# Two mixture layers computed by routed expert groups in place of all experts for all tokens, around a causal attention layer

## The reference

```
x = x + 0.5 * mixture(norm(x))      # router over 4 experts, the best 2 count
x = x + attention(norm(x))          # causal, linear (no softmax), 16 heads of 16
x = x + 0.5 * mixture(norm(x))      # the same weights again

mixture(h):
  g = softmax(layer_norm(h) @ router_w.T); top2_w, top2_idx = top_k(g, 2), renormalized
  hid = relu(layer_norm(h @ w1[e]) * ln_g + ln_b)         # per expert, 256 -> 512
  out = sum over the two experts of top2_w * (hid @ w2[e])    # 512 -> 256
  return layer_norm(out) * on_g + on_b
```

## Time and profile before

| | us |
|---|---|
| device time, median of 3 runs (lowest, highest) | 1240.89 (1239.82, 1241.86) |
| the profiled execution: span from first to last instruction | 1236.4 |
| TensorE matmul busy, 8694 matmuls | 1140.2 (92%) |
| VectorE busy | 948.3 (77%) |
| GpSimd busy | 672.0 (54%) |
| ScalarE busy | 512.8 (41%) |

### The profile page before, as it was taken

The page is one execution under the profiler, slowest core; times in us unless marked ns, Lnnn a source line. Parts: engine busy times, 40 slices in busy tenths (PEclk is TensorE's granted clock), DMA queues, the critical chain, the costliest instruction groups (busy, mean ns, idle before and its releaser), DMA issues.

```text
span 1236.4 us, 25066 instructions
## 1 busy us (share of the span) xinstructions
PE 1140.2 (92%) x8694; PEld 731.9 (59%) x8694; DVE 948.3 (77%) x2150; ACT 512.8 (41%) x878; POOL 672.0 (54%) x1039
## 2 busy tenths in 40 slices
PE   4669799999999999889999999889999999999996
PEld 4335456656566566656666666556566665666664
DVE  5678787887978878657777777578879787797875
ACT  4353324233342424456665666442333424334131
POOL 2365546454565544498778777543555654546360
PEclk9789989999999999999999999899999999999998
DMA  9002000000000000000000000000000000000000
GB/s 286 4 1 69 1 1 2 1 2 1 0 0 0 1 2 1 19 18 15 11 13 18 17 18 18 1 2 2 17 1 18 1 19 18 0 17 1 19 18 17
DMA packets 29037, 20.69 MB, mean 17 GB/s; under 512 B 7812, under 2 KB 27784, under 8 KB 28808
## 3 DMA queue, kind: packets, MB, share of 16 engines
q1 hardware_dynamic: 24112, 18.36, 5.4%
q10 hardware_dynamic: 4824, 1.07, 0.5%
HBM read 11.03 MB, written 4.19 MB: 12 GB/s over the span
## 4 chain that ended last, share of the span: by engine, by line
PE 48%; DVE 19%; issue 16%; POOL 10%; ACT 4%; DMA 2%; DVEq 1%; ACTq 0%; POOLq 0%
PE bank L1547 7%; PE bank L1549 6%; PE bank L1548 6%; DVE area L674 5%; DVE area L682 4%; PE bank L1532 4%; PE bank L1534 4%; PE bank L1533 4%; DVE area L655 4%; PE bank L1506 4%; POOL area L487 3%; PE bank L1555 2%; PE bank L1557 2%; PE bank L1556 2%; DMA betas<-in_L_ffn_ln_b_dram 2%
## 5 line engine op out<-in xcount | busy, mean ns | idle before, releaser
L1256 ACT ACTIVATE area<-area 128x512 f16<-128x512 f32 x256 | 160.9, 630 | 387.9 <-DVE area L674 386.1
L1547 PE MATMUL bank<-w2h,area 128*128 128x256 f16 x1024 | 281.3, 275 | 12.9 <-DVE area L693 7.2
L1548 PE MATMUL bank<-w2l,area 128*128 128x256 f16 x1024 | 280.5, 274 | 0.0
L1549 PE MATMUL bank<-w2h,area 128*128 128x256 f16 x1024 | 280.5, 274 | 0.0
L674 DVE SCALAR_TENSOR_TENSOR area<-area,betas,bank 128x512 f32<-128x512 f32 x256 | 189.9, 743 | 46.0 <-PE bank L1534 37.6
L682 DVE SCALAR_TENSOR_TENSOR area<-area 128x512 f16<-128x512 f32 x256 | 188.7, 737 | 20.3 <-ACT area L1256 17.1
L1532 PE MATMUL bank<-hTh,w1h 128*128 128x512 f16 x512 | 195.5, 382 | 6.7 <-DVE area L674 6.7
L1533 PE MATMUL bank<-hTl,w1h 128*128 128x512 f16 x512 | 195.1, 381 | 0.0
L1534 PE MATMUL bank<-hTh,w1l 128*128 128x512 f16 x512 | 194.9, 381 | 0.0
L696 DVE SCALAR_TENSOR_TENSOR area<-bank,coef,area 128x256 f32<-128x256 f32 x192 | 92.1, 482 | 79.3 <-PE bank L1549 78.1
L487 POOL TENSOR_TENSOR area<-area 128x512 f16<-128x512 f32 x96 | 119.9, 1274 | 45.1 <-ACT area L1300 44.9
(11 more groups left out here) (233 smaller groups left out, 2109.6 us busy)
## 6 DMA issues: line engine op xcount, KB each, us to landing
X<-in_L_attn_x_dram SPq DMA_DIRECT2D x8, 512.0 KB, 7.1
area<-area SPq DMA_DIRECT2D x128, 32.0 KB, 2.0
out_dram<-X SPq DMA_DIRECT2D x7, 512.0 KB, 2.9
area<-in_L_ffn_w_dram SPq DMA_DIRECT2D x4, 512.0 KB, 9.9
X<-in_L_ffn_w_dram SPq DMA_DIRECT2D x2, 1024.0 KB, 15.7
area<-in_L_ffn_ln_g_dram ACTq DMA_DIRECT2D x1, 1024.0 KB, 6.1
out_dram<-X SPq DMA_DIRECT2D x4, 128.0 KB, 1.7
area<-in_L_attn_Wq_dram SPq DMA_DIRECT2D x1, 256.0 KB, 9.2
```

Source lines behind the costliest of these rows:

```text
L1256: act.activation(Rh[:, e % 2, m, :], V[:, a % NV], ACT.Relu).then_inc(s_Rh, 1)
L1547: pe.matmul(dst, Rh[:, e % 2, k, rows], w2h[:, e, k, :], start=(k == 0), stop=False)
L1548: pe.matmul(dst, Rh[:, e % 2, k, rows], w2l[:, e, k, :], start=False, stop=False)
L1549: last = pe.matmul(dst, Rl[:, e % 2, k, rows], w2h[:, e, k, :], start=False, stop=(k == HC - 1))
```

## The change

Each mixture layer is now done in two **groups** of 16 token tiles (2048 tokens). Tokens are **routed** first: rows are normalized, transposed, multiplied by the router, the two best experts chosen, and a running count per expert (a matmul with a triangle of ones, `prefix`, and `carry`) gives each token a slot in its two experts' regions of a DRAM tensor `slots_in`. GpSimd **scatters** each token tile's rows (two f16 halves, 1 KB a token) twice by indirect DMA. An expert's region is then cut in slot tiles of 256 rows. A group always has 19 slot tiles (16 + 4 - 1), 38 a layer; the tables `etab` and `rtab` say which expert and which rows each one has, and TensorE and the sync engine read them into a register (`value_load`). Per slot tile the sync engine issues two transposing loads and one plain load, TensorE computes the Gram products, `layer1` and `layer2` for the one expert with 256 columns per matmul, and the result is scaled by the inverse deviation and stored to `slots_out`. Afterwards GpSimd **gathers** each token tile's two results by indirect DMA, ScalarE and VectorE weight and sum them, and `token_out` normalizes and adds to `X`.

Routing of the second group is woven into the slot tiles of the first (one token tile in the first and second of each three, two in the third), bringing out of the first group into those of the second; bringing out of the second group stands behind the last slot tile, and in the second layer routing of the first group stands ahead of the first. In the preparation the rows are routed between the steps of the weights. The offset ln_b goes into `w1` as a row of its own (the row 128 of `w1` is subtracted from all rows and freed, its place takes the deviation), so `hidden` and `std_spread` are gone. `partition_all_reduce` is replaced by a transpose, a reduction and a small matmul. `attention` waits for all 32 token tiles (`c_x`), its preparation stands ahead of it, and all loops are unrolled. A DMA waits for earlier uses of its buffer as before.

The core of the diff (helpers of one operation and the attention's renamed arguments are left out):

```diff
+    GT = 16
+    NJ = GT + E - 1
+    NP = 2 * NJ
+    AHEAD = 5
+    R_HS, R_HT, R_SD, R_Y, R_C = 3, 5, 5, 4, 3
...
+            def load_slots(p):
...
+                row = sp.value_load(rtab[0:1, G % 2, J:J + 1], min_val=0, max_val=(E - 1) * REG + GT * P - S2)
+                wait(sp, b_A, 2 * (p - R_HT + 1))
+                for k in range(2):
+                    sp.dma_start_transpose(hT[:, p % R_HT, :, k * P:(k + 1) * P],
+                                           slots_in[G % 2][bass.ds(row + k * P, P), :]).then_inc(l_hT[p % R_HT], 16)
+                wait(sp, b_h2, p - R_HS + 1)
+                sp.dma_start(hs[:, p % R_HS].rearrange("p s c d -> p s (c d)"), ...
...
+            def scatter(i):
...
+                for k in range(2):
+                    pool.indirect_dma_start(slots_in[G % 2],
+                                            bass.IndirectOffsetOnAxis(spos[:, Q % 2, k, j:j + 1], 0),
+                                            hrow[:, t].rearrange("p c d -> p (c d)"), None
+                                            ).then_inc(sc_h[Q % GQ], 16)
+            def pair_std(p):
+                pool.wait_ge(b_ve, p + 1)
+                pool.tensor_tensor(stds[:, p % R_SD], vare[...], expo[...], ALU.pow).then_inc(b_sd, 1)
+            def gather(i):
...
+                wait(pool, c_acc, i - R_C + 1)
+                for k, d in enumerate((yA, yB)):
+                    pool.indirect_dma_start(d[:, i % R_C], None, slots_out[G % 2], ...
...
+            def relu_low(p, k):
+                dve.wait_ge(b_Rh, 2 * p + k + 1)
+                ms = slice(2 * k, 2 * k + 2)
+                dve.scalar_tensor_tensor(out=Rl[:, p % 2, ms]..., in0=bank[k][:, :], scalar=0.0,
+                                         in1=Rh[:, p % 2, ms]..., op0=ALU.max, op1=ALU.subtract).then_inc(b_Rl, 1)
...
+                # vector engine, per slot tile p of group g
+                for p in range(p0, p0 + NP):
+                    if g == G and k < GQ and r == 0:
+                        quad_factors(Q1 + k)
+                    if g == G and 1 <= k <= GQ and r == 1:
+                        place(Q1 + k - 1)
+                    if 1 <= out <= GT:
+                        token_out(i0 + out - 1)
+                    variances(p + 2)
+                    for t in routed(j):
+                        row_low(i0 + GT + t)
+                    relu_low(p, 0)
+                    if g == G and 1 <= k <= GQ and r == 0:
+                        logits(Q1 + k - 1)
+                    if 0 <= out < GT:
+                        token_sum(i0 + out)
+                    std_parts(p + 2)
+                    if g == G and 1 <= k <= GQ and r == 0:
+                        choose(Q1 + k - 1)
+                    if g == G and r == 2 and k + 1 < GQ:
+                        quad_norm(Q1 + k + 1)
+                    relu_low(p, 1)
+                    twice_low(p + 3)
+                for t in range(GT):
+                    token_sum(i0 + GT + t)
+                    if t >= 1:
+                        token_out(i0 + GT + t - 1)
...
+            def layer1(p, k, e):
+                pe.wait_ge(b_sdr, p + 1)
+                wait(pe, b_Rl, 2 * (p - 1) + k + 1)
+                for m in range(2 * k, 2 * k + 2):
+                    o = bank[k][:, m % 2 * S2:(m % 2 + 1) * S2]
+                    for c in range(KC):
+                        pe.matmul(o, w1h[c][m][:, bass.ds(e, 1), :], a[:, c], start=(c == 0), stop=False)
+                        pe.matmul(o, w1h[c][m][:, bass.ds(e, 1), :], a[:, KC + c], start=False, stop=False)
+                        last = pe.matmul(o, w1l[c][m][:, bass.ds(e, 1), :], a[:, c], ...
...
+                # tensor engine, per slot tile p
+                    e[p + 2] = expert(p + 2)
+                    grams(p + 2, e[p + 2])
+                    layer1(p, 0, e[p])
+                    std_T(p + 1, done)
+                    layer2(p - 1, 0, e[p - 1])
+                    if g == G and 1 <= k <= GQ and r == 1:
+                        prefix(Q1 + k - 1)
+                    layer1(p, 1, e[p])
+                    row_T(...)
+                    layer2(p - 1, 1, e[p - 1])
+                    router(...)
...
             def attention():
-                pe.wait_ge(s_V, NA * NBLK)
+                pe.wait_ge(c_x, NT)
+                pe.wait_ge(l_att, 16 * 8)
...
+                pool.wait_ge(c_x, NT)
+                pool.memset(qx..., 0.0).then_inc(a_zero, 1)
...
+                rs(0)
+                add_bias(0)
```

More of the change, by code:

```diff
@@ L567, in attention @@
+                key_low(0)
                 for g in range(NG - 1):
-                    score_low(0, 0, g)
-                post_tile(NBLK - 1, 1, 0, 0, at)
-                start = at.at
-                per = N_RS_ATT
-                extra = 2 * (TB - 1)
-                def body(n, par, last):
-                    first = isinstance(n, int) and n == 0
-                    at = Steps(pool, pool_done, start if first else n * per + (start + extra))
+                    score_low(0, g)
+                for n in range(NBLK):
+                    last = n == NBLK - 1
@@ new lines, in all_max, with chain @@
+            def all_max(k):
+                dve.wait_ge(p_mt, k + 1)
+                step(dve.tensor_reduce(mxr[:, k:k + 1], max_bank(k)[0:4, 0:P], AX.X, ALU.max))
+                dve.tensor_scalar(mxd[:, k, :], identf[0:4, 0:4], mxr[:, k:k + 1], None, ALU.mult).then_inc(p_md, 1)
+                dve.wait_ge(p_mb, k + 1)
+                step(dve.tensor_copy(mxa[:, k, :], max_bank(k)[:, P:P + 4]))
+            def chain(Q):
+                logits(Q)
+                choose(Q)
+                place(Q)
@@ new lines, in weights @@
+                router_weights()
+                quad_norm(0)
+                quad_norm(1)
+                quad_factors(0)
+                quad_factors(1)
+                centre(0)
+                row_low(0)
+                row_low(1)
+                centre(1)
+                row_low(2)
+                row_low(3)
+                logits(0)
+                choose(0)
+                place(0)
+                centre(2)
+                row_low(4)
+                row_low(5)
+                centre(3)
@@ L1091, in body @@
[L1091 to L1099 removed]
+                            last_score_low(c + 1)
                         mask_kv(c)
@@ L1178, in centre, with weights @@
+            def weights():
                 def centre(e):
@@ L1470, in first_block_and_weights, with expert @@
-                last.then_inc(p_rt, 1)
-                router(0, 0, 0)
-                w1_gram(3)
-                pe.wait_ge(p_gl, E)
-                pe.wait_ge(p_rc, 2)
-                for j in range(NU):
-                    gram(0, 0, j)
+                prefix(2)
+                w1_gram(3)
+                quad(3)
+                prefix(3)
+                maxima_T(2)
+                maxima_all(2)
+            def expert(p):
+                G, J = group(p)
+                if J == 0:
+                    pe.wait_ge(r_tab, G + 1)
+                return pe.value_load(etab[0:1, G % 2, J:J + 1], min_val=0, max_val=E - 1)
```

2168 lines of the change are left out of this document (1110 added, 1058 removed).

## The result

The changed kernel takes **1294.42 us** (median of 5 runs, 1286.06 to 1295.76) beside 1240.89: ratio 1.042, 95% interval [1.039, 1.045], **slower**. The forecast was 1167.

What follows compares the result with a forecast made beforehand. TensorE, 92% busy and bound by matmul columns, was taken as the limit. Preparation 118, layers 272 twice, tails 58 twice, attention 31 + 285, second routing 66 and last store 2 gave 1162; with 4.5, 1167 us, range 1080 to 1330.

Steps and rivals of the forecast that it cites:

- The slot tile on TensorE, 6.45: Per slot tile: 56 matmuls of 256 columns at 0.110 us plus four transposes, together 6.45 us of TensorE.
- Register reads, 0.3 a tile: Reading the expert into a register per slot tile: between nothing and 2.0 us, taken as 0.3.
- Indirect DMAs, 1.3: Each GpSimd scatter or gather of 128 token rows, 128 a layer: 1.3 us, bounded by 0.67 and 2.6.
- Rival (b): GpSimd's indirect DMAs cost more: from 1.92 us each the kernel is slower than before, at 2.6 it takes 1350; chance 0.17.
- the same tile on VectorE: VectorE's work per slot tile: 3.8 us, 6.9 with routing in first groups, 6.1 with bringing out in second.
- With 0.15 for coupling, that makes 13 tiles at 7.6, 6 at 7.0: First-group slot tiles, with register read and coupling; with 19 second-group tiles at 6.9, 272 us a layer.
- Rival (c): VectorE becomes the bound: lumps between the `relu_low` halves make a slot tile 8.5 us, 1269 in all; chance 0.13.
- Second routing, 66: Second layer's first routing, hidden by nothing: routing, scatters, landing, load and filling take 66 us.
- GpSimd's 32 scatters and 8 powers are 50 us, ending near 56: Within the second layer's uncovered routing: GpSimd's chain of 50 us, beside VectorE's 41, followed by landing, load and filling.
- Preparation, 118: Start to first `layer1`: VectorE 75 us, idle 27, engine hops 8, filling 8; 118 us against 63 before.
- Tail, 58 and a last store of 2: Bringing out 16 token tiles after each layer's last slot tile: 58 us, twice; plus 2 for the kernel's last store.
- Attention, 31 + 285: Exposed startup of attention after the last token tile, 31 us, and its loop without woven Gram work, 285.

Runs made afterwards that it cites:

- third set: Later set of kernels run together on one chip, without late waits; the changed kernel, unedited, took 1251.50 us there, 1.010 of before.
- first two edits: Each alone against the changed kernel: second-group scatters spread over three slot tiles, 1244.61 us; VectorE's woven routing work moved behind `relu_low`, 1235.52 us.
- h1: Changed kernel with the second layer's first-routing scatters issued behind the whole routing and 32 plain GpSimd DMAs in their old places: 1314.92 us.

## Why the prediction was wrong

By the profiled executions the 122 us over the sum are 42 of late waits (recorded against third set) and 80 without them: preparation 26, first groups 24, second routing 15, tails 15, second groups 9, and attention 8 the other way. Without late waits the kernel is 12 us slower than before, so had any one of the first four terms held, it would have been no slower. More than one step failed, then:

- **The slot tile on TensorE, 6.45**: right. Second groups begin at 6.5 Gram to Gram.
- **Register reads, 0.3 a tile**: nothing to be seen at 6.5, where TensorE reads well ahead of need. In the first groups, where the short router matmuls leave its queue empty just ahead of the Gram product, it does show, near the size that I gave it: 4.3 us in the first one. One of these reads begins at 256.49, the matmuls ahead of it end at 256.78, and the Gram product starts at 257.35.

```profile
L1641 PEldq TENSOR_LOAD <-etab x76: 296/301/793, 125.8 to 1188.0; - x76
...
PE bank L1652 <- issue: 4.3, 9, 0.6
```

- **Indirect DMAs, 1.3**: right, 0.98 busy and 0.30 of gap. Rival (b), which began at 1.92, did not happen; beside a busy VectorE the longest took 1.94, and no 3.1 was seen. GpSimd held VectorE instead: the step "the same tile on VectorE" priced `token_out` and `row_low` at their undisturbed time. That is the 5 us of each second group and 8 of the preparation.
- **"With 0.15 for coupling, that makes 13 tiles at 7.6, 6 at 7.0"**, 7.4 on average: even without late waits the first group takes 8.07 a tile. Rival (c) had the place right, lumps ahead of `relu_low`, at 8.5 for all tiles; it is 8.1 to 8.9 in first groups alone. But VectorE is no bound there, and my sum for it was too high: 13 tiles at 6.9 and 6 at 3.8 make 112 us, and it was busy 96 of the group's 153.

```profile
144.00:297.00 153.00, 134.42 (x1297) 112.31 (x1296) 95.91 (x375) 72.91 (x145) 59.09 (x58) 0.97 0.48 130
```

What I compared were sums (6.9 of 7.1), not what stands ahead of what. `place` waits 3.96 us for `prefix` with `variances` behind it; `tables` takes 3.7 us while `layer2` waits 4.0 for the `relu_low` behind it:

```profile
239.76 0.18 DVE L730 COPY pre<-bank 128x20 f32<-128x20 f32 x1 [3.96 <-PE bank L1589]
...
279.58 0.37 PE L1689 MATMUL bank<-w2h,area 128*128 x1 [4.01 <-DVE area L825]
```

Reordering alone gave 16 us, 10 of them at `tables`.
- **Late waits**: in no step and no rival, 32 to 43 us, and the reason that the record says 4% and not 1%. What brings them about stays open.
- **Second routing, 66**: 81 without late waits. The first scatter starts 17 us after attention, which I had laid beside VectorE's 41; then GpSimd's 32 x 1.27 = 40.6 and the powers between them run to 65, and landing and filling take the rest. "GpSimd's 32 scatters and 8 powers are 50 us, ending near 56" began its count too early.
- **Preparation, 118**: 143. VectorE was busy 88, not 75, of which 8 are the held `row_low`; idle it was 55, not 43.
- **Tail, 58 and a last store of 2**: 63 and 6.5. The bound was named rightly, the power and the wait in every other token (0.4 a token) were too small. The last store was not looked into; in pairs it takes 3.0.
- **Attention, 31 + 285**: 308, right within 3%. Its 31 is a slip: the terms add up to 30.

The range held the time, but by luck: its upper part was there for rivals (b), which did not happen, and (c), which did in part, and not for late waits or a longer preparation. Slower had been given 0.34.

## What to carry to other kernels

Where two in-order engines are both 90% full by count, walk the order: for each wait that a woven step brings, what stands behind it, and when is that due? An engine that is busy 63% of a stretch held the other one there. Moving work in the order and between engines, with the powers of the tails in pairs, gave 56 us here, at the same columns. A phase that hid beside other work (bringing out, routing) costs its full chain once it stands alone, counted from its first dependence, not from its longest engine. And run the unedited kernel in every set before an edit gets credit: by the third set's 1251.50, 43 of the 50 and 59 us that the first two edits seemed to give were the set's.

## What was not expected of the hardware

- While GpSimd issued scatters in a row, ScalarE and VectorE went on 2 to 8 us after TensorE's matmuls had ended by the trace, with TensorE running or idle, and TensorE's semaphores were raised as late. The condition held for a whole set, as far as was run: four of the six had it, the recorded one among them, and one of the three on one chip. What decides that was not found. Plain DMAs from GpSimd did not show it, in the one execution (h1) that had both.
- GpSimd's elementwise operations on 128x512 or 128x256 held VectorE's two-input operations to the end of the whole row of them: 8.75 us instead of 0.84 beside eight, 2.04 instead of 0.48 beside two.
- A stall of 4.0 us is paid a second time by the clock. Windows over the tile with `tables` (stall, right behind it, later): TensorE has 24 matmuls in 5 us at granted clock 0.50, which is 1.2 GHz, and 48 at 2.4 GHz.

```profile
274.00:279.00 5.00, 0.94 (x10) 0.45 (x7) 3.72 (x23) 1.19 (x2) 3.88 (x5) 0.92 0.51 145
279.60:284.60 5.00, 5.00 (x24) 3.51 (x25) 3.27 (x13) 0.47 (x1) 3.05 (x4) 0.50 0.29 111
287.00:292.00 5.00, 5.00 (x48) 4.22 (x46) 3.62 (x13) 1.99 (x4) 1.04 (x1) 1.00 0.53 183
```
